# Moving VectorE's reciprocals to other places in the batches of a second attention layer

## The reference

```python
x = L0_attn_x                                  # (2, 1024, 128)
xn = layernorm(x)
s = L0_attn(xn, ...)                           # 16 heads of 64, attention over the heads of a token
g = silu(L0_ffn(xn, ...))                      # 15 experts, top 2, one shared convolution
x = x + s * g
xn = layernorm(x)
s = L1_attn(xn, gamma, w_qkv, w_out)
g = silu(L1_ffn(xn, ...))                      # 128 -> 512 -> 512 -> 512 -> 128
x = x + s * g

def L1_attn(x, gamma, w_qkv, w_out):           # the part that matters here
    xn = rms_norm(x, gamma)
    q, k, v = heads_of(xn @ w_qkv)             # 16 heads of 64
    attn = softmax((q * 64 ** -0.5) @ k.T)     # over 1024 keys
    return concat_heads(attn @ v) @ w_out
```

## Time and profile before

| | |
|---|---|
| median of three runs | 1207.56 us |
| profiled execution, its own time | 1208.63 us |
| its span from first to last instruction | 1206.8 us |
| TensorE busy | 1151.7 us, 95% |
| VectorE busy | 843.3 us, 70% |
| ScalarE busy | 597.7 us, 50% |
| GpSimd busy | 775.8 us, 64% |

### The profile page before, as it was taken

How to read it: one execution, slowest core, us unless ns; L and a number is a source line. 1 busy time by engine, 2 the same in 40 slices (tenths; PEclk the granted TensorE clock), 3 DMA queues, 4 the chain that set the end, 5 groups by cost and what they waited for, 6 DMA issues and landing times.

```text
span 1206.8 us, 21785 instructions
## 1 busy us (share of the span) xinstructions
PE 1151.7 (95%) x8892; PEld 731.1 (61%) x8892; DVE 843.3 (70%) x1086; ACT 597.7 (50%) x930; POOL 775.8 (64%) x495
## 2 busy tenths in 40 slices
PE   7999999998887899999999999999999999899997
PEld 6899999876664445454444544544445445457776
DVE  4765886565566577787777777778778787865553
ACT  1543334546553645555554555546555455554342
POOL 3565776753433678878878788898888888840000
PEclk9998999998998999999999999999999999999999
DMA  6000000020000020000000000000000000000000
GB/s 206 2 2 2 3 2 2 2 72 1 1 1 1 1 95 2 1 1 1 1 1 1 1 1 1 2 1 1 1 1 1 1 1 1 1 1 10 9 9 9
DMA packets 6978, 13.65 MB, mean 11 GB/s; under 512 B 1744, under 2 KB 4176, under 8 KB 6496
## 3 DMA queue, kind: packets, MB, share of 16 engines
q1 hardware_dynamic: 6096, 11.66, 2.9%
q10 hardware_dynamic: 784, 0.61, 0.2%
HBM read 11.22 MB, written 1.05 MB: 10 GB/s over the span
## 4 chain that ended last, share of the span: by engine, by line
PE 85%; DVE 8%; ACT 3%; issue 3%; ACTq 1%; POOL 0%; DVEq 0%; POOLq 0%
PE o_ps L1335 19%; PE mx_ps L1294 8%; PE ha_banks L494 7%; PE st_ps L1314 5%; PE st_ps L1317 5%; PE st_ps L1320 5%; PE bank L1693 3%; PE pj_ps L1246 3%; PE pj_ps L1265 3%; PE bank L1695 3%; PE bank L1694 3%; PE pj_ps L1257 2%; PE ha_banks L558 2%; PE ha_banks L511 2%; PE pj_ps L1240 2%
## 5 line engine op out<-in xcount | busy, mean ns | idle before, releaser
L1609 POOL TENSOR_TENSOR acc<-acc,prob 128x1024 f32<-128x1024 f32 x192 | 466.3, 2429 | 77.4 <-ACT prob L1456 68.5
L1518 DVE TENSOR_REDUCE mx_part<-mx_ps 128x2 f32<-128x1024 f32 x251 | 300.4, 1197 | 145.6 <-PE mx_ps L1294 145.6
L1456 ACT ACTIVATE prob<-st_ps 128x1024 f32<-128x1024 f32 x256 | 248.6, 1023 | 226.3 <-PE st_ps L1320 226.3
L1335 PE MATMUL o_ps<-prob,v_cur 128*64 128x512 f32 x1024 | 244.8, 599 | 0.0
L1294 PEld LDWEIGHTS mx_ps<-k_hi,q_hi 64*128 64x128 f32 x502 | 47.2, 184 | 142.3 <-issue 98.1
L1294 PE MATMUL mx_ps<-k_hi,q_hi 64*128 64x512 f32 x502 | 122.8, 485 | 8.8 <-DVE mx_part L1518 8.4
L1335 PEld LDWEIGHTS o_ps<-prob,v_cur 128*64 128x64 f32 x1024 | 65.5, 136 | 97.6 <-issue 90.8
L1534 DVE RECIPROCAL rden<-rden 128x128 f32<-128x128 f32 x128 | 120.3, 942 | 2.6 <-ACT rden L1420 2.6
L1609 POOL TENSOR_TENSOR acc<-prob 128x1024 f32<-128x1024 f32 x32 | 76.0, 2375 | 51.9 <-PE pj_ps L1242 31.2
L1320 PE MATMUL st_ps<-q_hi,d_lo 64*128 64x512 f32 x512 | 101.3, 391 | 0.0
L752 POOL TENSOR_TENSOR ha_wide<-ha_pt,ha_own 128x512 f32<-128x512 f32 x64 | 73.8, 1185 | 8.6 <-ACT ha_pt L709 8.6
(11 more groups left out here) (364 smaller groups left out, 2207.3 us busy)
## 6 DMA issues: line engine op xcount, KB each, us to landing
h_w<-in_h SPq DMA_DIRECT2D x2, 1024.0 KB, 8.0
w_raw<-in_w SPq DMA_DIRECT2D x8, 192.0 KB, 3.6
x<-in_x SPq DMA_DIRECT2D x4, 256.0 KB, 6.4
head_wkv<-in_wkv SPq DMA_DIRECT2D x1, 1024.0 KB, 10.6
out<-fin SPq DMA_DIRECT2D x4, 256.0 KB, 2.3
m_w<-in_m SPq DMA_DIRECT2D x3, 256.0 KB, 2.8
sel_raw<-in_sel SPq DMA_DIRECT2D x1, 576.0 KB, 11.3
ha_head_pos<-in_pos ACTq DMA_DIRECT2D x2, 256.0 KB, 7.8
```

Of the source, the lines that this page charges most:

```text
L1335: mm = pe.matmul(o_ps[rows(h), :], v_cur[:, m % 2, j, rows(h)], prob[:, (16 * m + slot) % RING, h, :], start=(j == 0), stop=(j == KT - 1), ...
L1456: act.activation(prob[:, n % RING, :, :], st_ps[:, slot % 2, :, :], ACT.Exp, scale=SCALE).then_inc(s_exp, 1)
L1518: dve.reduce_max(mx_part[:, :, i, keys:keys + 1], maxima_banks(q, n), AX_X).then_inc(s_mxr, 1)
L1609: pool.tensor_tensor(total, old, new, ALU.add).then_inc(s_acc, 1)
```

## The change

`INVERT` says in which batch a piece of which half is inverted, as (half, piece, offset of the step). Before, it is keyed by the batch, and each batch has one reciprocal at one place: behind the first maximum and the addition to `y`, ahead of the second maximum. After, it is keyed by batch and place. Place 0 is the old one. Place 1 is behind the second maximum and the unit's low parts, ahead of the normalization. Batches 0, 2, 4, 6 and 7 have their reciprocal at place 1, batch 1 at place 0, batch 5 at both, and batch 3 has none. The normalization of half 1 moves from batch 5 to batch 6. The work is the same, and so are the queues of the other engines.

```diff
-    INVERT = {6: (0, 0, 0), 7: (0, 1, 0), 0: (0, 2, -1), 1: (0, 3, -1),
-              2: (1, 0, -1), 3: (1, 1, -1), 4: (1, 2, -1), 5: (1, 3, -1)}
+    INVERT = {(6, 1): (0, 0, 0), (7, 1): (0, 1, 0), (0, 1): (0, 2, -1), (1, 0): (0, 3, -1),
+              (2, 1): (1, 0, -1), (4, 1): (1, 1, -1), (5, 0): (1, 2, -1), (5, 1): (1, 3, -1)}
@@ def vector(dve, m, b):
-        vector_invert(dve, m, b)
+        vector_invert(dve, m, b, 0)
         for name in NORMS_AT.get((m, b), ()):
             e.vector_norm(dve, LAST, name)
         at_b = before(m, b)
         if second:
             vector_maxima(dve, *second)
         if at_b and at_b[1][0] == "tr":
             vector_spread_max(dve, *at_b)
         if at_b and at_b[1][0] == "qk":
             vector_low(dve, *at_b)
+        vector_invert(dve, m, b, 1)
         if b == 1 and m >= 1:
             vector_normalize(dve, m - 1, 0)
-        if b == 5 and m >= 1:
+        if b == 6 and m >= 1:
             vector_normalize(dve, m - 1, 1)
@@ the end, interleaved with the last network
                 t2.vector(dve, STEPS, 2)
-                t2.vector(dve, STEPS, 3)
                 end.vector_hidden(dve, 0, 1, 1)
                 t2.vector(dve, STEPS, 4)
                 end.vector_hidden(dve, 0, 1, 2)
                 t2.vector(dve, STEPS, 5)
+                t2.vector(dve, STEPS, 6)
                 end.vector_hidden(dve, 0, 1, 3)
```

More of the change, by code:

```diff
@@ L1523, in vector_maxima, with vector_invert @@
                .then_inc(s_row, 1)
-    def vector_invert(dve, m, b):
-        half, n, ahead = INVERT[b]
+    def vector_invert(dve, m, b, place):
+        if (b, place) not in INVERT:
+            return
+        half, n, ahead = INVERT[b, place]
         q = m + ahead
```

## The result

The changed kernel is slower: 1217.26 us median of 12 runs (1212.79 to 1223.15) against 1208.79 us of the kernel before, now with 12 runs (1204.00 to 1216.41). The ratio is 1.0064, 95% interval 1.0035 to 1.0093, or 7.7 us. The prediction had the direction, but said 1233.4 us, and its range began at 1217.0 against a median before of 1207.56; the time scaled by the ratio lies at 1215.3.

What follows compares the result with a forecast made beforehand. TensorE sets the pace, VectorE matters where a first maximum must be reduced before `mx_ps` is rewritten. 5.6 + 12.5 + 0.8 + 6.7 + 0.9 - 0.7 = 25.8 us gave 1233.4 us; own range 1228 to 1239, whole range 1217 to 1240.

Steps and rivals of the forecast that it cites:

- Batch 0 into 1: Batch 0's reciprocal, now behind `d_all`, makes batch 1's first maximum 0.40 us late; 14 x 0.40 = 5.6 us.
- Batch 1 into 2: Half 0's normalization waits for GpSimd's addition, making batch 2's first maximum 0.89 us late; 14 x 0.89 = 12.5 us.
- The rival with the won lock: Batch 1's normalization goes ahead of GpSimd's addition; the 12.5 term falls away, 13.3 remain: 1220.9 us; chance 0.20.
- a normalization of 0.7 us in batch 1: Sign named beforehand: the forecast is wrong if batch 1's normalization lasts 0.7 us; it expected about 2.9.
- The Trainium skill's rule: VectorE with two SBUF inputs and GpSimd reading SBUF exclude each other; first starter holds the ports; used for batch 1.
- Batches 2 and 3: Batch 2's reciprocal behind `q_lo` uses 0.86 of 0.98 us idle ahead of batch 3's first maximum; cost 0.
- Batch 4 into 5: Batch 4's reciprocal behind `d_all` makes the next first maximum 0.06 us late; 14 x 0.06 = 0.8 us.
- Batch 6 into 7: Half 1's normalization waits for an addition; batch 7's first maximum 0.39 us late in 8 steps, 0.60 in six: 6.7 us.
- The end: Two reciprocals instead of one ahead of the last normalization and `act13`: 0.9 us; half 0's last normalization counted as 0.
- The gain in step 1: In step 1 batch 0 the reciprocal no longer stands ahead of `xr`, for which TensorE waited 0.66: -0.7 us.
- Elsewhere the second maxima are earlier: Outside step 1 batch 0, second maxima are reduced 0.18 to 0.5 us earlier, which nothing waits for; no gain counted.

Runs made afterwards that it cites:

- e1_b0_early: Changed kernel with batch 0's reciprocal put back ahead of the second maximum; ratio to the kernel before 1.0010, step 43.19 us (m = 2 to 7) against 43.53.
- e2_norm5: Changed kernel with the normalization of half 1 back at the end of batch 5, reciprocals as changed; ratio to the kernel before 1.0004, step 43.13 us.
- e4_norm6_only: Kernel before with only the normalization of half 1 moved from batch 5 to batch 6; ratio to the kernel before 1.0091, steps 43.37 and 43.6 us.
- e6_cut14: Changed kernel with GpSimd's part of d_lo (SLOT_CUT 12 to 14) two slots later; ratio to the kernel before 1.0028, step 43.13 us.
- e5_tr_late: Kernel before with only the reciprocals of batches 2, 3 and 7 moved to place 1; 1205.61 us, ratio to the kernel before 0.9954, step 42.73 us.
- e9_rpad10: Changed kernel with an added reciprocal of 128 by 10 ahead of batch 1's normalization; one run, 1236.00 us, step 44.45 us (m = 2 to 7).
- e12_rpad1: Changed kernel with an added reciprocal of 128 by 1 ahead of batch 1's normalization; one run, 1235.45 us, step 44.43 us (m = 2 to 7).

## Why the prediction was wrong, step by step

*Batch 0 into 1*, 0.40 us a step: 0.34 (`e1_b0_early`). The mechanism is right. What I shifted was the reduction's start, and what TensorE waits for is its end. A reduction that VectorE had waited for takes 1.23 us, one that was already queued takes 1.16: both lengths stood in the earlier trace rows. The start moves by 0.41, the end by 0.34.

*Batch 1 into 2*, 12.5 us: 0. This is the step that failed. The prediction put the normalization at 737.49 and the addition at 737.46 and took the lock as lost. By the 0.06 too much in the step above it was on the wrong side; in the trace it starts 0.01 to 0.03 us ahead of the addition and wins in every step. The mechanism, its size (0.92 a step against 0.89 forecast) and, for what was run without a memset, the way in which it is decided are right, as the reciprocals of one to 24 columns show. The forecast hung on 0.03 us, worked out from rows to 0.01 each, and gave the losing side 0.62 against 0.20. The rival with the won lock said 1220.9 us; that mechanism is what happened, and the prediction had named its sign, a normalization of 0.7 us in batch 1. A number with a cliff of 12 us at 0.03 us deserved even chances, and a check of both ends of the shift.

*The Trainium skill's rule* (SBUF — State Buffer, section "SBUF: two separate sides"), that whoever starts first holds the shared ports for the whole instruction, agrees with the trace where the pads are reciprocals (behind by 0.05: 2.86 us) and in the changed kernel (ahead by 0.02: 0.68 us). It does not explain the memsets by the normalization's own start.

*Batches 2 and 3*: 0, right.

*Batch 4 into 5*, 0.06 a step: 0.01 (TensorE's pairs at 760.00 and 761.83, 1.83 apart, 1.82 before). The same error, the reduction's 1.16 instead of 1.23.

*Batch 6 into 7*, 0.39 and 0.60 a step, 6.7 us: 0.40 and 0.62, about 7.0 us (`e2_norm5`, `e4_norm6_only`, `e6_cut14`). Right, and now the largest cost of the change. One number in its reasoning was wrong without effect: the normalization's forecast start, 721.61, lies 1.49 us behind 720.12 and not 1.1.

*The end*: 0.81 for `act13` against 0.86. And the last step's normalization of half 0, which stood 0.11 behind an addition, fell to the other side: 0.69 us instead of 2.83, which gave TensorE 0.79 back, so that the end is as long as before.

*The gain in step 1*: 0.73 for `xr` as forecast. Not foreseen: `xr_lo` then starts 0.7 us ahead of an addition, where it had started 0.13 behind one and waited for its end; it takes 0.68 us instead of 2.79, and TensorE gets 1.6 us more.

*Elsewhere the second maxima are earlier, "which nothing waits for"*: wrong. In batches 3 and 7 the output projection waited for `q_max`. I had seen that wait and taken it for the matmuls in front. It is 0.10 us in each of the 28 batches, 2.8 us, as `e5_tr_late` shows.

The sum from the measured terms: 14 x 0.34 = 4.8, lock 0, 0.1, 7.0, 0.8 - 0.8 at the end, -0.7 and -1.6 in step 1, -2.8: 6.8 us. That is 6.5 less than the 13.3 of the won lock: 5.2 are the three gains not foreseen (2.8, 1.6, 0.8), the rest mainly the two ends that move less than their starts. With the 1.7 of the clock in step 15, for which the prediction had no term, it is 8.5. The result is 7.7 us, with an interval from 4.2 to 11.2, which holds both sums.

## What to carry to other kernels

Where two engines exclude each other from a port instruction by instruction, list the pairs that meet in the steady loop with their starts, and treat any pair closer than the error of your working (0.06 us here, against a distance of 0.03) as a coin toss with both prices. Shift ends, not starts, through a chain: the same reduction took 1.16 us when it was queued and 1.23 when VectorE had waited for it. And before writing that nothing waits for an earlier result, compare each wait with the same wait at a place where it cannot bind.

## What the runs showed of the hardware

A VectorE reciprocal of 128 by 1 ahead of one normalization made fourteen steps 14 us longer, while a memset of 128 by 256 at the same place cost nothing (steps of 43.50 us). The memset, which has no input, kept GpSimd's addition waiting (3.13 us instead of 2.37), also where its recorded start lay 0.07 us behind the addition's; the reciprocal of any width did not. How early GpSimd asks for the port, against its recorded start, is left open, but the traces bound it. With no memset in front, the normalization won at 0.006 us ahead (step 9 of the changed kernel) and at 0.003 behind (the last step of `e9_rpad10`: 0.69 us, the addition 2.96), and lost at 0.036 behind (step 10 of `e12_rpad1`: 2.88 us).
